# Two experts found by a sort of the eight logits and a search for their places, and the lists of turns written anew

## The chip, the cores and the metric

One core of one Trainium2 chip runs the whole program. The metric is the device time of one execution in microseconds (us). A core has five engines that run side by side, each with its own instruction queue: TensorE (PE, matrix products and transposes into PSUM), VectorE (DVE), ScalarE (ACT, exp, gelu, copies with a scale), GpSimd (POOL) and SyncE (SP, which issues the DMAs). They wait for each other by semaphores only.

## The reference, cut to what matters

Four layers stand one behind the other, each with a cross attention (16 heads, a context of 154 tokens) and a feed-forward part; the residual stream `x` is 4 batches x 1024 rows x 256. The feed-forward parts of layers 1 and 3 are mixtures of eight small experts, of which each row uses two:

```python
# layer 1
logits = x @ gate_w.T                       # [rows, 8]
scores = softmax(logits)
weights, idx = top_k(scores, 2)             # the scores themselves are the weights
base = x @ W_lin.T + b_lin
t = einsum('nd,nkdr->nkr', x, left[idx])    # rank 4 for each expert
out = base + sum_k weights[k] * (t[k] @ right[idx[k]])

# layer 3
probs = softmax(t @ gate_w.T)               # [rows, 8]
topw, topi = top_k(probs, 2)
topw = topw / sum(topw)
weights = sum(one_hot(topi, 8) * topw)      # each row's weight for each expert
out = einsum('te,etd->td', weights, out_e)  # out_e: a gated unit with a rank-16 part for each expert
```

A tie goes to the expert with the lower number.

## The kernel before, in words

The 4096 rows are cut into 16 pieces of 256. Four streams `S[0]` to `S[3]` each own one piece of a batch at a time and carry it through all four layers; then they store it and load the piece of the next batch. A stream's data stay in SBUF, 128 partitions x 2 rows. PSUM has eight banks: four form the `quad`, in which attention scores are made for one stream at a time, the others are handed out bank by bank.

The work of a stream is cut into some 30 kinds of stages (`norm`, `turn`, `qp`, `sc`, `mx`, `s2`, `ex`, `pv`, `out`, `gate1`, `top1`, `tl`, `lin`, ...). A stage has a part on each engine that it needs. Within an engine the instructions run strictly in the order in which they were written, so the order of the stage parts of the four streams is what can be chosen. That order is fixed at build time by two things:

- `TURN` holds one string of digits for each engine: the k-th digit says from which stream the k-th stage part of this engine comes (1688 digits for PE, 1190 for ACT, 1206 for DVE, 592 for POOL, 34 for SP).
- `parts` holds a planned duration of every stage on every engine (`pe`, `dve`, `act`, `pool`, in ns). `orders()` walks the strings with these durations. Because the strings give the streams, the durations decide nothing of the order within an engine: they decide which bank a stage gets, and how many `fill` matmuls go into the PE queue. Where the plan sees PE wait for more than 450 ns, it puts a `fill` there: matmuls of an identity (L992) whose result nobody reads, sized to three quarters of the planned wait.

The stages that the change touches are these.

Layer 1. `gate1` on PE (L1370) makes base, the eight logits and the rank-4 products in one go, 296 columns for each of the two row groups, in two banks. `gate1` on DVE takes the largest logit of each group (L1968, `tensor_reduce` from PSUM) and subtracts it (L1971); that lets ACT take the exp of the eight (L1659). `top1` on DVE then finds the two experts, as a one-hot over eight for each: `first` (L1950 to L1953) marks the places with the value 0, multiplies them by the row 8, 7, ..., 1 (`rev`, a slice of the tile `w_first`), takes the largest and compares it with `rev` to get the first expert alone, and then puts that place far below the rest; L1981 takes the largest of what is left; `second` (L1959 to L1962) does the same marking for it. Each of these operations waits for the one before it by the semaphore `d_own` (the helper `own`). The rest of `top1` (L1983 to L1991) adds the two one-hots, weighs the exps, divides by their sum and multiplies the rank-4 products, into the tile `tl`. `tl` on PE (L1378) transposes that, ACT copies it (L1669), `lin` on PE (L1386) multiplies it by `right` into the two banks of base, and `lin` on DVE (L2001) adds all of it to `x`.

Layer 3. `gate3` on PE (L1442) makes only the logits, 16 columns in one bank. `gate3` on DVE takes the largest (L2065), subtracts it (L2066), runs `first` and takes the second largest (L2068), which lets ACT take one exp (L1664). `top3` on DVE runs `second` and then four operations that make the two weights (L2077 to L2080). `mw` on POOL (L948, L950) spreads one-hots and weights over 128 columns, PE transposes them (L1453) and ACT copies them to SBUF (L1705); then come `exa`, eight rounds `h1`, `h2`, `hw`, `back` on all engines, `e3` (L2118, L2121) and `f3` (L1508).

Each of the four stages runs 16 times: four streams, four batches.

Of the kernel before, what the change touches and what calls it, by code (L numbers as in the profile page):

```python
# [29 lines left out]
def build(nc, d, out):  # L30
# [5 lines left out]
    with ctx:  # L36
# [20 lines left out]
        def res(name, shape, dt=f32):  # L57
# [5 lines left out]
        FMQ, GATES, FMQB, SGN, FMV, FMVB, NEGC, SELC, TM, BD2, REV, BQ, BK, NW, UPB, G3 = (  # L63
# [3 lines left out]
        gates, fmqb, sgn, fmv, fmvb, negc, selc, tm, bd2, rev, nw, upb = (  # L67
            GATES, FMQB, SGN, FMV, FMVB, NEGC, SELC, TM, BD2, REV, NW, UPB)
# [105 lines left out]
        for i in range(NS):  # L174
# [64 lines left out]
            s.gs = [s.g8[:, k, :, :] for k in range(6)]  # L239
            s.tops = [s.sm[:, 8 + k, 0:2] for k in range(6)]  # L240
# [16 lines left out]
        def parts(name, of):  # L257
# [12 lines left out]
                   "down": 700, "gate1": 620, "top1": 2800, "lin": 800, "q1": 2390, "w1": 660, "am": 2170, "fin": 830,  # L270
                   "q2": 1420, "w2": 400, "gate3": 1440, "top3": 1515, "exa": 1600, "h1": 885, "h2": 800, "e3": 1120,
# [106 lines left out]
        def turns(s):  # L378
# [35 lines left out]
            for b in range(4):  # L414
# [161 lines left out]
                "0323023032323232002020221221202201003303100331331302121212012121032021202302322013221321303213300323"  # L576
                "1301202030201203123121301310012002011321013210203231300232202201321300103133233030122013122010010230"
                "2102113102311212330202020301322131210301301300233033203020232102101013001010031303313212102121100211"
                "2021302303230000032313003000000000000032001312230032210131211112111111111111111212101331103021202302"
                "0201221022223022312222212210200222210102211032313012323333233323333333233333233130302322122302013032"  # L580
                "3032003213213301203131030210103123013100230021021312310113102032312300220220321310302301331032310320"
                "1012210031020210233211103321102010222030221323101301131003003323303020232102101201300101003331301231"
                "2101211210103123203203021030302000000030002000100300032013200202132321010301112111111111111111111133"
                "2113021203202022012210222212223231222122102002122202012103231303212333233323332333230333333332022331"
                "3221230323031031230313102301303201020310120312313010203002102321311311021230031302022022032131030230"
                "3313310320201121020031020210132312110323110201022203022132310301301130120303323023203201210101031000"
                "1303033130121120121121012021302302301300200203003003030103100300000002022300322101213011112111111111"
                "1111112111020131312320202030212210232021232122012002222222222100122123031303133232133333333333323323"
                "3323133023202212323032013032032123010213030210331032101031023130120200310231211301131020323123002202"
                "2103231030203331331203020112102003102021013231211021112330202020301322131213031012300303032223030230"  # L590
                "1201010130010103033130312112012112101202120323020310000300020303000030003003020130022100322321013121"
                "1121121111111111111111133113212232222222222222222222232232232333333333333333333333333333",
            "ACT":
                "0001030032122312020023003233011123211200310031202212201213133033010322021213213233032001202101310031"
                "3030222102102100133331212321200022021031133011302232303012100020113032300230111312201010130320223210"
                "1021023120330331000303300000000000120121323211211111111111131212102130020320021212212323222222200302"
                "2201010313122323313333333303333310202232210230310220213012303101332113213302300203210311301013303202"
                "2102120010313321231321020022032301311301032122300213010002103133020302113112010103213022203312110301"
                "2032302130303010300000000001002021213231002101111111130111121113203220232122121222232222200302212001"
                "3103123223313333330303333332201222323103012013211033200321302113123302300202330131113030103022210210"  # L600
                "2010333132231211200022023301311301032212300213010020130233021030111312110300321023023212110202103230"
                "1303000030303010011000000202323211211101131121111111121020032203012212321232222002202222231001330132"
                "1332323133333333333001202233223012002121201230103031332112310332302020331011310013303202201210201033"
                "3123213211200022032301131101302322303121002001013203230030113112010130231023022312110022102303103000"
                "300303003000010200102231231211211211211111111311133222222222223222222323333333333333333333",
            "DVE":
                "3233203213023230232020232020313231023103120202223200111122121233223223220023023321130303001212110020"
                "0332121020303110032131201122030320213122313130200023302123301000110103112310312032200212102230210301"
                "1332323130310132100322003212301303200021300300000010003031100121211122111111111112121030312130232200"
                "2220232212212212212003200212130333032333332333323323113331122223322030303310103300331221110202003312"  # L610
                "0120131030023213120211003202131221331020233003203200100111001313101213032002211202230210320112333332"
                "1313010120032320013123302101000002000302000300303101012021011221111111111111132321302301220220221222"
                "1322122132220020021132003332332333232333333331132321122322333000331010330013322111202033002121001301"
                "0032323120121103020231221331102023300230320010011100132301312101322002121223021030110333233231310101"
                "2300223001231203130020100200330031003100000001221111212111111111112210013231033222002202121322122222"
                "2120230200303201133333333332332332331123321213223223030003110333001332211120200033120120131000323231"
                "2012101032023122133110202302030123301000110113021321013232012002122030210301133233321331010120022330"
                "0212130100021033000020300303000301012210221111121111211111111331233222222222222222233232333333333333"
                "333333",
            "POOL":  # L620
                "0100100102301132012123200203133102210302313201100322012302113020323101301232002013011332010200303201"
                "2300001000311121111211112200231213022220221233030233331032333213123022300103132013210203301211030230"
                "2120323121300032310113200210301332210103020013321100002000031120110121011112232312221232012223300210"
                "2333323333132123023102003131032321030032110023212101032313000232130112320010321032130103200021301300"
                "1200300011211212111110202301132320222221230302033333231332132312102230010330322110303120103012320121"
                "03231302002313101232201003013132010232000103000301200031112211111211123222232222233333333333",
            "SP": "0300030102300000123000010230001023",
# [1105 lines left out]
        def dve_program(e):  # L1733
# [551 lines left out]
```

## Time and profile before

| | us |
|---|---|
| median of 3 runs | 2492.91 (2492.24 to 2493.57) |
| the profiled execution's own time | 2491.67 |
| its span, first to last instruction | 2489.6 |
| PE busy | 2375.2 |
| DVE busy | 1325.7 |
| ACT busy | 1144.9 |
| POOL busy | 854.1 |

The span is some 2 us shorter than the execution's own time. Busy times are unions of the instructions of one engine; each engine also waits, and only waits of the engine that bounds a stretch cost time. The program falls into four batches, each of which passes layers 0 to 3 with the four streams a little apart; so every view that goes over the whole span mixes stretches with different limits.

### The profile page before, as it was taken

What the parts mean: (1) busy time and instruction counts of PE and PEld (TensorE: products, weight loads), DVE (VectorE), ACT (ScalarE), POOL (GpSimd) and SP (SyncE); (2) the same over time, 40 slices, a digit from 0 to 9 for tenths busy, and PEclk for the clock granted to TensorE, in tenths of its full rate; (3) what the DMA queues carried; (4) which work ended last, traced back from release to release, by engine and by line L of the source; (5) the groups of instructions that cost most, each with busy time, mean ns of one, the idle gap of its engine ahead of it and who ended that gap; (6) DMA issues with size and microseconds to landing.
All of it is one profiled execution on the core that took longest, in us unless ns stands there. A gap on an engine that the chain in (4) does not pass through costs nothing.

```text
span 2489.6 us, 51976 instructions
## 1 busy us (share of the span) xinstructions
PE 2375.2 (95%) x21666; PEld 1601.6 (64%) x21666; DVE 1325.7 (53%) x2974; ACT 1144.9 (46%) x1756; POOL 854.1 (34%) x1546
## 2 busy tenths in 40 slices
PE   8999989999999988999999998899999999899999
PEld 4676544777777644567777754467777765447777
DVE  6544776545433577644543367764544346865442
ACT  5534567323344548723325445762323545683211
POOL 1332332434332332334432233333433223334342
PEclk9999999999999999999999999999999999999999
DMA  3200002000000000000000000000000000000000
GB/s 137 89 12 1 13 19 84 1 9 10 10 10 13 13 2 15 2 9 8 3 9 21 1 13 1 13 1 10 9 10 10 13 2 13 1 2 1 1 9 9
DMA packets 16614, 37.86 MB, mean 15 GB/s; under 512 B 1472, under 2 KB 11520, under 8 KB 15360
## 3 DMA queue, kind: packets, MB, share of 16 engines
q1 hardware_dynamic: 16384, 34.55, 4.0%
q8 instruction: 174, 2.85, 0.5%
q14 instruction: 56, 0.46, 0.1%
HBM read 29.78 MB, written 4.19 MB: 14 GB/s over the span
## 4 chain that ended last, share of the span: by engine, by line
PE 74%; DVE 9%; ACT 9%; issue 5%; POOL 2%; DMA 0%; DVEq 0%; ACTq 0%; POOLq 0%
PE P L1475 9%; PE P L1262 5%; PE P L1508 5%; PE P L1359 5%; PE P L1484 4%; PE P L1476 4%; PE P L1493 4%; PE P L1334 4%; PE P L1240 4%; PE P L1153 4%; PE P L1346 4%; ACT ET L1633 3%; DVE mx L1882 3%; PE P L1269 3%; PE P L1149 2%
## 5 line engine op out<-in xcount | busy, mean ns | idle before, releaser
L1882 DVE TENSOR_REDUCE mx<-P 128x8 f32<-128x1232 f32 x256 | 367.2, 1434 | 210.8 <-PE P L1158 86.1
L1475 PE MATMUL P<-Et,w 128*128 128x256 f32 x1024 | 265.7, 382 | 0.1
L1475 PEld LDWEIGHTS P<-Et,w 128*128 128x128 f32 x1024 | 192.1, 190 | 60.2 <-issue 33.4
L1926 DVE SCALAR_TENSOR_TENSOR x<-P,w_first,x 128x512 f32<-128x512 f32 x96 | 71.8, 748 | 273.9 <-PE P L1359 98.9
L1587 ACT ACTIVATE Et<-x,sm 128x256 f32<-128x256 f32 x256 | 139.2, 594 | 156.4 <-POOL sm L885 155.7
L1633 ACT ACTIVATE ET<-P 128x2048 f32<-128x2048 f32 x96 | 180.2, 1877 | 40.7 <-PE P L1252 20.4
L1711 ACT ACTIVATE gu<-P 128x256 f32<-128x256 f32 x128 | 49.0, 383 | 299.7 <-PE P L1476 280.0
L1153 PE MATMUL P<-KB,R 32*128 32x308 f32 x1536 | 155.7, 474 | 20.6 <-DVE mx L1882 10.6
L932 POOL TENSOR_TENSOR R<-R 128x512 f32<-128x512 f32 x48 | 60.8, 1268 | 319.9 <-DVE R L1918 319.9
L2098 DVE SCALAR_TENSOR_TENSOR gu<-gu,P 128x256 f32<-128x256 f32 x128 | 53.8, 420 | 215.8 <-ACT gu L1711 215.6
L1240 PE MATMUL P<-R,KB 32*128 32x256 f32 x2048 | 162.8, 405 | 3.6 <-DVE mx L1882 3.6
L1262 PE MATMUL P<-ET,VB 128*32 128x256 f32 x2048 | 146.1, 392 | 13.9 <-ACT ET L1633 5.9
L879 POOL TENSOR_SCALAR sm<-mv 128x2 f32<-128x2 f32 x96 | 18.4, 192 | 395.9 <-DVE mv L1877 394.1
L1476 PE MATMUL P<-gu,b 128*128 128x256 f32 x512 | 152.4, 380 | 0.0
L903 POOL TENSOR_TENSOR x<-x,w_bias 128x512 f32<-128x512 f32 x112 | 141.8, 1268 | 28.7 <-ACT Et L1587 28.6
L992 PE MATMUL P<-identb 128*128 128x512 bf16 x486 | 134.8, 389 | 6.6 <-POOL mg L852 4.6
L1484 PE MATMUL P<-gu,b 128*128 128x256 f32 x512 | 134.4, 385 | 0.0
L1346 PE MATMUL P<-Et,wup 128*128 128x256 f32 x512 | 124.1, 388 | 0.1
L956 POOL TENSOR_TENSOR Et<-Et,gu 128x512 f32<-128x512 f32 x48 | 60.9, 1268 | 173.8 <-DVE Et L2105 173.8
L1240 PEld LDWEIGHTS P<-R,KB 32*128 32x128 f32 x2048 | 81.6, 187 | 59.0 <-issue 33.7
L1508 PE MATMUL P<-w_w,R 128*128 128x256 f32 x512 | 118.3, 385 | 0.8 <-DVE R L2121 0.4
L1359 PE MATMUL P<-wdn,R 128*128 128x256 f32 x512 | 114.6, 382 | 1.8 <-ACT R L1653 1.8
(290 smaller groups left out, 4968.2 us busy)
## 6 DMA issues: line engine op xcount, KB each, us to landing
kvw<-in_wkv SPq DMA_DIRECT2D x12, 672.0 KB, 4.0
x<-in_x SPq DMA_DIRECT2D x16, 256.0 KB, 2.8
out<-x SPq DMA_DIRECT2D x16, 256.0 KB, 2.1
w<-in_w SPq DMA_DIRECT2D x2, 1024.0 KB, 8.6
w<-in_wexp SPq DMA_DIRECT2D x1, 1028.0 KB, 8.8
w_w<-in_wcon SPq DMA_DIRECT2D x1, 1024.0 KB, 11.0
w_w<-in_m3t SPq DMA_DIRECT2D x1, 1024.0 KB, 6.7
w<-in_w1q SPq DMA_DIRECT2D x1, 1024.0 KB, 10.0
```

The lines of the kernel that those rows point to most:

```text
L903: e.tensor_tensor(s.x[:], s.x[:], gb[:, k:k + 1, :].broadcast_to([128, 2, 256]), ALU.add).then_inc(s.g_x, 1)
L1153: t = e.matmul(quad[:, g, 0:2 * NK], s.QT[G4[g], u, rows], K[G4[g], 2 * u:2 * u + 2, :], start=True, stop=l >= 2)
L1240: e.matmul(quad[:, g, cols], K[G4[g], j, 0:128], s.QT[G4[g], j if l == 0 else u, :], start=a == 0, stop=False, skip_group_check=True)
L1262: t = e.matmul(o[G4[q], :], of(q), ET[:, g, 256 * a:256 * a + 256], start=start, stop=False, skip_group_check=True)
L1346: t = e.matmul(o[:, 256 * (j % 2):256 * (j % 2) + 256], wup[:, c, 128 * j:128 * j + 128], s.xT[:, c, :], start=c == 0, stop=c == 1)
L1359: t = e.matmul(o[:, 256 * i:256 * i + 256], s.hT[:, j, 128 * i:128 * i + 128], wdn[:, j, :], start=j == 0, stop=j == 7)
L1475: e.matmul(o, wm[:, c, js], s.xT[:, c, :], start=n == c == 0, stop=False, skip_group_check=True)
L1476: t = e.matmul(o, bm[:, js], U[:, 2 * n, :], start=False, stop=False, skip_group_check=True)
L1484: t = e.matmul(P[:, k, 256 * n:256 * n + 256], bm[:, js], U[:, 2 * n + 1, :], start=False, stop=n == 1, skip_group_check=True)
L1508: e.matmul(o, s.G[:, j, rows], w2[:, j, :], start=j == 0, stop=False)
L1633: e.activation(ET[:].rearrange("p g c -> p (g c)"), quad.rearrange("p g c -> p (g c)"), ACT.Exp, bias=mb1[:, b:b + 1] if l == 1 else 0.0). ...
L1882: e.tensor_reduce(s.mx[:, i, :, 2 * u:2 * u + 2], quad[:, :, 0:2 * NK].rearrange("p g (a k) -> p g a k", a=2), AX.X, ALU.max).then_inc(q_d, 1)
```

## The change

The chain of comparisons goes. In its place stand two instructions of VectorE for each row group: `max` writes the eight values of a row in falling order, and `max_index` writes the places at which given values stand. One comparison of the places with the row 0, 1, ..., 7 (`kth`, in the place of `rev`) then makes both one-hots of both groups at once. The places are written into the slot 3 of the tile `g8`, read as unsigned integers (`s.at`).

```diff
-            def first(s):
-                g, m, sh = s.gs, s.tops, [128, 2, 8]
-                rv = rev[:].unsqueeze(1).broadcast_to(sh)
-                own(e.scalar_tensor_tensor(out=g[3], in0=g[0], scalar=0.0, in1=rv, op0=ALU.is_equal, op1=ALU.mult))
-                own(e.tensor_reduce(m[3], g[3], AX.X, ALU.max))
-                own(e.tensor_tensor(g[1], rv, m[3].unsqueeze(2).broadcast_to(sh), ALU.is_equal))
-                own(e.scalar_tensor_tensor(out=g[5], in0=g[1], scalar=-1e38, in1=g[0], op0=ALU.mult, op1=ALU.add))
-            def second(s):
-                g, m, sh = s.gs, s.tops, [128, 2, 8]
-                rv = rev[:].unsqueeze(1).broadcast_to(sh)
-                own(e.tensor_tensor(g[3], g[5], m[2].unsqueeze(2).broadcast_to(sh), ALU.is_equal))
-                own(e.tensor_tensor(g[3], g[3], rv, ALU.mult))
-                own(e.tensor_reduce(m[3], g[3], AX.X, ALU.max))
-                own(e.tensor_tensor(g[2], rv, m[3].unsqueeze(2).broadcast_to(sh), ALU.is_equal))
+            def ranked(s, of):
+                for i in range(2):
+                    e.max(s.gs[5][:, i, :], of[i]).then_inc(d_own, 1)
+                e.wait_ge(d_own, C.up(d_own, 2))
+            def found(s, of):
+                for i in range(2):
+                    e.max_index(s.at[:, i, :], s.gs[5][:, i, :], of[i]).then_inc(d_own, 1)
+                C.up(d_own, 2)
+            def chosen(s):
+                e.wait_ge(d_own, C.at(d_own))
+                sh = [128, 2, 2, 8]
+                own(e.tensor_tensor(s.g8[:, 1:3, :, :], kth[:].unsqueeze(1).unsqueeze(1).broadcast_to(sh),
+                                    s.at[:, :, 0:2].rearrange("p i k -> p k i").unsqueeze(3).broadcast_to(sh), ALU.is_equal))
             def gate1(s, k0, k1):
-                g, m = s.gs[0], s.tops[0]
+                g = s.gs
+                logits = [P[:, k, 256:264] for k in sorted((k0, k1))]
                 e.wait_ge(s.p_d, C.up(s.p_d))
-                for i, k in enumerate(sorted((k0, k1))):
-                    e.tensor_reduce(m[:, i:i + 1], P[:, k, 256:264], AX.X, ALU.max).then_inc(d_own, 1)
-                e.wait_ge(d_own, C.up(d_own, 2))
-                for i, k in enumerate(sorted((k0, k1))):
-                    t = e.tensor_scalar(g[:, i, :], P[:, k, 256:264], m[:, i:i + 1], None, ALU.subtract)
+                ranked(s, logits)
+                for i in range(2):
+                    t = e.tensor_scalar(g[0][:, i, :], logits[i], g[5][:, i, 0:1], None, ALU.subtract)
                 t.then_inc(s.d_a, 1)
                 C.up(s.d_a)
+                found(s, logits)
             def top1(s, k0, k1):
                 lo = [P[:, k, 264:296] for k in sorted((k0, k1))]
                 g, m = s.gs, s.tops
-                e.wait_ge(s.d_a, C.at(s.d_a))
-                first(s)
-                own(e.tensor_reduce(m[2], g[5], AX.X, ALU.max))
-                second(s)
+                chosen(s)
                 own(e.tensor_tensor(g[5], g[1], g[2], ALU.add))
                 e.wait_ge(s.a_d, C.up(s.a_d))
...
             def gate3(s, k):
                 g, m = s.gs, s.tops
-                logits = P[:, k, 0:16].rearrange("p (i n) -> p i n", i=2)
+                logits = [P[:, k, 8 * i:8 * i + 8] for i in range(2)]
                 e.wait_ge(s.p_d, C.up(s.p_d))
-                own(e.tensor_reduce(m[0], logits, AX.X, ALU.max))
-                own(e.tensor_tensor(g[0], logits, m[0].unsqueeze(2).broadcast_to([128, 2, 8]), ALU.subtract))
-                first(s)
-                e.tensor_reduce(m[2], g[5], AX.X, ALU.max).then_inc(s.d_a, 1)
+                ranked(s, logits)
+                found(s, logits)
+                e.tensor_tensor(m[2], g[5][:, :, 1], g[5][:, :, 0], ALU.subtract).then_inc(s.d_a, 1)
                 C.up(s.d_a)
             def top3(s):
                 m = s.tops
-                e.wait_ge(s.d_a, C.at(s.d_a))
-                second(s)
+                chosen(s)
                 e.wait_ge(s.a_d, C.up(s.a_d))
```

The planned durations of the four stages on DVE change with it, and all five strings of `TURN`:

```diff
-                   "down": 700, "gate1": 620, "top1": 2800, "lin": 800, "q1": 2390, "w1": 660, "am": 2170, "fin": 830,
-                   "q2": 1420, "w2": 400, "gate3": 1440, "top3": 1515, "exa": 1600, "h1": 885, "h2": 800, "e3": 1120,
+                   "down": 700, "gate1": 900, "top1": 1700, "lin": 800, "q1": 2390, "w1": 660, "am": 2170, "fin": 830,
+                   "q2": 1420, "w2": 400, "gate3": 800, "top3": 950, "exa": 1600, "h1": 885, "h2": 800, "e3": 1120,
...
-            "SP": "0300030102300000123000010230001023",
+            "SP": "0300030012300000123000001230002013",
```

The order of the stages of one stream on one engine stays as it was; what changes is how the streams are laid between each other. Counted from the strings, with each stage followed by its stream and its number in it, these stage parts stand at another place than before: 924 of 1688 on PE, 612 of 1190 on ACT, 617 of 1206 on DVE, 382 of 592 on POOL and 6 of 34 on SP, spread over all four batches. Nine in ten of these are moved by one to five places, a few by up to 30. Between `gate1` and `tl` of the same stream PE had 84 stages of other streams in all 16 cases together, and has 78 after.

## Rows read from the trace of the kernel before

**Rows 1.** The page: busy time by engine, and PE in 40 slices.
```profile
PE 2375.2 (95%) x21666; PEld 1601.6 (64%) x21666; DVE 1325.7 (53%) x2974; ACT 1144.9 (46%) x1756; POOL 854.1 (34%) x1546
...
PE   8999989999999988999999998899999999899999
```

**Rows 2.** Windows of 100 us: us, busy (and count) by engine, granted PE clock, DMA.
```profile
500.00:600.00 100.00, 98.87 (x696) 73.65 (x689) 45.85 (x111) 31.35 (x57) 39.27 (x61) 1.00 0.04 12
...
800.00:900.00 100.00, 94.31 (x987) 59.13 (x985) 56.19 (x139) 52.01 (x75) 27.97 (x62) 1.00 0.03 8
900.00:1000.00 100.00, 88.72 (x985) 49.70 (x985) 75.06 (x161) 68.85 (x83) 33.73 (x73) 1.00 0.03 10
```

**Rows 3.** The same windows for the fill matmuls, line 992 alone: the sum.
```profile
sum 2500.00, PE 134.83 PEld 44.67; mean PE 5.39 PEld 1.79
```

**Rows 4.** The page: the chain that ended last, by engine.
```profile
PE 74%; DVE 9%; ACT 9%; issue 5%; POOL 2%; DMA 0%; DVEq 0%; ACTq 0%; POOLq 0%
```

**Rows 5.** Timeline of DVE in one `top1` of batch 2: start, us, instruction.
```profile
1451.48 0.17 DVE L1951 TENSOR_REDUCE sm<-g 128x2 f32<-128x16 f32 x1
...
1453.14 0.17 DVE L1983 TENSOR_TENSOR g<-g 128x16 f32<-128x16 f32 x1
```

**Rows 6.** Groups of DVE by line and shape: busy, mean ns of one | idle before.
```profile
L1950 DVE SCALAR_TENSOR_TENSOR g<-g,w_first 128x16 f32<-128x16 f32 x32 | 10.8, 339 | 0.7
L1960 DVE TENSOR_TENSOR g<-g,w_first 128x16 f32<-128x16 f32 x32 | 9.3, 291 | 1.1
L1962 DVE TENSOR_TENSOR g<-w_first,sm 128x16 f32<-128x16 f32 x32 | 8.3, 260 | 1.1
L1952 DVE TENSOR_TENSOR g<-w_first,sm 128x16 f32<-128x16 f32 x32 | 7.6, 237 | 1.1
L1991 DVE SCALAR_TENSOR_TENSOR R<-P,sm,g 128x32 f32<-128x32 f32 x32 | 6.6, 247 | 0.6
L1953 DVE SCALAR_TENSOR_TENSOR g<-g 128x16 f32<-128x16 f32 x32 | 5.6, 175 | 1.1
L1968 DVE TENSOR_REDUCE sm<-P 128x1 f32<-128x8 f32 x32 | 3.7, 157 | 5.1 <-PE P L1370 5.1
```

**Rows 7.** Timeline of DVE: `gate1` of stream 0 in batches 1 to 3, counted from 0.
```profile
844.59 0.24 DVE L1968 TENSOR_REDUCE sm<-P 128x1 f32<-128x8 f32 x2 [0.74 <-PE P L1370]
...
1449.91 0.24 DVE L1968 TENSOR_REDUCE sm<-P 128x1 f32<-128x8 f32 x2 [0.71 <-PE P L1370]
...
2048.95 0.24 DVE L1968 TENSOR_REDUCE sm<-P 128x1 f32<-128x8 f32 x2 [0.74 <-PE P L1370]
```

**Rows 8.** Waits of all engines: who <- whom, us in total, times, longest.
```profile
ACT g L1659 <- DVE g L1971: 22.8, 13, 3.9
```

**Rows 9.** The chain in order of time, at two `top1`: start, us, what.
```profile
236.08 0.98 DVE g L1950
...
2097.03 0.09 DVE g L1950
```

**Rows 10.** Groups of PE by line: the transpose behind `top1`.
```profile
L1378 PE MATMUL P<-ident,R 128*64 128x128 f32 x16 | 4.5, 284 | 7.0 <-DVE R L1991 5.4 <-ACT R L1647 1.4
```

**Rows 11.** Waits of PE alone, columns as in rows 8.
```profile
PE P L1153 <- ACT ET L1633: 7.9, 18, 2.1
```

**Rows 12.** Timeline of all engines at the last `gate3` and `top3`.
```profile
2417.57 0.17 DVE L2065 TENSOR_REDUCE sm<-P 128x2 f32<-128x16 f32 x1
...
2419.05 1.13 PE L1493 MATMUL P<-gu,w_a 128*128 128x512 f32 x2
...
2420.01 2.32 PE L992 MATMUL P<-identb 128*128 128x512 bf16 x10
...
2421.12 0.17 DVE L2077 TENSOR_SCALAR sm<-sm 128x2 f32<-128x2 f32 x1
...
2421.80 0.42 DVE L2118 SCALAR_TENSOR_TENSOR R<-P,gu 128x256 f32<-128x256 f32 x1
```

**Rows 13.** A window of 10 us in batch 3, columns as in rows 2.
```profile
2130.00:2140.00 10.00, 6.38 (x76) 2.40 (x69) 8.53 (x28) 4.41 (x6) 3.59 (x9) 0.83 0.00 0
```

More of the change, by code:

```diff
@@ L581, in build @@
[L581 to L585, printed above, removed]
@@ new lines, in build @@
+                "0232303230323232202002220120222101000331003331013313112212120122302120232032122013220132302313300323"
+                "1310320210230201021321301310021002011321013210203231300232202210231030103133233032021013122010010230"
+                "2101211301213212330202020301322131213010130030230333030202321012021013000110303310321231212011121010"
+                "2103230230320000303210003000300300020030100022103032210121311121111121121111111111113310130021020203"
+                "2221021202212222321223022021200222210210211032313102323233323333323333333332033313023220322123032301"
@@ new lines, in build @@
+                "3032032031332130101321030210103120313100230021023211231011310032313020220220132303010230331331203102"
+                "1122100031020210312321103231120102202030221323101301110303003323303020232102102101300011030331301231"
+                "1201211201103213023020210302003200303000000130000000002321300230122132130111211111111111112111121133"
+                "1103021202030201222102220221212221232322012002222010212103230313323123323333233333230333233323221330"
+                "3022123032303103103120313321320301030210102132031310203002310231211311021320302310022022032131030230"
@@ new lines, in build @@
+                "3313312030201101221003102021031212310323112010230022021232310130101310320330320323023201012011031000"
+                "1303033130121120121121012021203203203130030003200030023000000300010030201320322101213011211101111111"
+                "1111121111133211301020320203221202102221223122102002222222221202201230113012312333323323333233333333"
+                "2333310330232212230210310312303213002312331303020310102031210301312012003032113011321020323130202202"
+                "2103231030230331132320301011220100310202102113231021112330202020301322131210303101203003323223030230"
@@ new lines, in build @@
+                "1201101030100130303313011212012112110202103230230230203003103003000230000000100030022301022321013121"
+                "1111211211111111111111133113212232222222222222222222222332232333333333333333333333333333",
+            "ACT":
+                "0000300212321213020023003203131111232012300312012210220213133033130021202132321233023002102101310031"
+                "3300222102102010133332123112200022021013130131302232303012100020113033020302113112010310231022202331"
+                "2110201032033031000303030000001200010022313211211112111231121111111300320002021221212232232222200302"
+                "2201013013212123333333333333033031202202232330102210231332013011032112313302300203231011310031303022"
+                "2012001203133123121321200022023130131301021232300213010002103133020302113112010130231022203312101032"
+                "1032301203000330030100010000000223211123211011111121112111131230203020011222212222322232200022231001"
+                "1303312332123333333033033323210202232303101210132133201302031123123303200230233101113030130202202110"
+                "2003133123213211200022032130131301032312200213010200130323020130111312101300321023202312110202102303"
+                "1033030030030001200000001021323211230111110111121111211130230020233211222122222002222032221003031122"
+                "1233313333033333333301022232210321031102120321023303301213123032302010323011310031303022201210201033"
+                "1322313121200022023101331101302232303012100200112303230030111312101300312023023212110202103203303013"
+                "030300002000011000002321231211112121111131112111132322222232222222222233333333333333333333",
@@ new lines, in build @@
+            "DVE":
+                "2332313023203232023202020302132310032130120322121223001121212233223223202203302323113300001122110020"
+                "0332121020313100023131201212030320212123313130200020323123301000110103112130132031202021022301203201"
+                "1333233213012310122003300123201033020002100310300300030001011202111221111121111121111033012130220222"
+                "3012221222302212212302000212303303233233333332333321131323112222332033003110330300133221112020200331"
+                "1020130100332321020121103022131221331020233002303201000111001313101213032010222102230120320113332332"
+                "1310310123003220031120121330020002030000030000033011012211122111111111111212103031210202322320022121"
+                "2221322122230200023210331303323333233233233331312321221323203300311030303013322111202033002121001310"
+                "0032323120121100320321122313102023300230320101001100132131021310322002121220301302110332333321310101"
+                "2030223002121320331010000203003000030003011001221211112111111111111200323133021202202202123122122222"
+                "2213020200201033332332313333323333321133311222232230330013130303003132121102000332121020131000323213"
+                "1202110230302112231310202330200123301000110103112320113220302021122030130121033233332131010120022330"
+                "0232032310120001130030003000000301102201221111121111111111211331232223222222222222233223333333333333"
@@ new lines, in build @@
+                "0210132321300320310132010210301232101330022001301030001020031121121111112202301120232220231223300233"
+                "2303332331123203121030103330232112030210310023211002312310320321301021320010310321201302032001330120"
+                "0001003011211211111120023231220022212322133002203333333312131202312230031030312103020313210012321230"
+                "02311032023130102230101203103321013022000310320100000301112211111111223223232222223333333333",
+            "SP": "0300030012300000123000001230002013",
@@ L2260 @@
         fm2, rows(np.concatenate([v["g_xattn"], v["g_ffn"]])), np.tile(v["L0_xattn_fm_b"], 8), sgn, spread(fmT, 8),
-        rows(v["L0_xattn_fm_b"]), negc, selc, tm, bd2, rows((8.0 - np.arange(8)).astype(np.float32)), bq, bk,
+        rows(v["L0_xattn_fm_b"]), negc, selc, tm, bd2, rows(np.arange(8).astype(np.float32)), bq, bk,
         v["L3_ffn_norm_w"].reshape(2, 128).T, v["L0_ffn_up_bias"].reshape(8, 128).T, kt(v["L3_ffn_gate_w"].T))], 1)
```

51 lines of the change are left out of this document (6 added, 45 removed).

## The prediction

> **What bounds the kernel now.** I read the page first, then windows of 100 us, then the chain, and last the single groups and timelines. PE is busy 95% of the span, DVE 53% [rows 1]. But PE's share is an average over unlike stretches: in layers 3 and 0 of a batch PE is full (98.87 of 100 us), in layers 1 and 2 it is busy 94.31 and 88.72 us while DVE rises to 56.19 and 75.06 [rows 2]. And part of PE's busy time is no work: the fill matmuls take 134.83 us over the whole program [rows 3], so that with the 114 us of idleness (2489.6 less 2375.2) some 249 us of PE's queue are not work. In layers 1 and 2 the end is therefore set by chains that run over DVE, ACT and PE in turn; DVE holds 9% of the chain that ended last [rows 4]. The change shortens DVE's part in layer 1, where that counts, and in layer 3, where PE is full and it mostly does not.
>
> **Layer 1, `top1`.** Nine instructions go: L1950 to L1953, L1981, L1959 to L1962. Each waits for the one before. From the start of L1951 to that of L1983 are eight such steps in 1.66 us [rows 5], 0.2075 us each, nine are 1.87 us. That is the quiet case. The four that read the tile `w_first` have means of 339, 291, 260 and 237 ns, against 175 for L1953, their like without it [rows 6]: they are held up now and then, by 107 ns in the mean. Four of them in a stage add 0.43 us. Removed: 2.30 us.
>
> Added, in `top1`: one comparison of 32 elements that reads `w_first` too. Its nearest rows are L1962 (260, with the hold-ups in it) and L1991 (247, 32 elements) [rows 6]; with the step's gap of some 35 ns I take 0.30 us, and for the doubled size and the hold-ups 0.10 more: 0.40 us. Ends: 0.21 (the quiet step) and 0.56, twice L1991 with its gap twice.
>
> Added, in `gate1`: the two `max` stand where the two reductions stood (L1968, 157 ns each from PSUM [rows 6]) and write eight values in place of one; I give the pair 0.05 us more. The two `max_index` are new work behind the subtraction. The trace of before has no such instruction. From below they are two small PSUM reads that don't wait for each other: not under zero, since they occupy the queue, and the pair L1968 takes 0.24 us together [rows 7], so 0.12 each. From above I allow four times the dearest mean of a small operation here, L1968's 157 ns: 0.63 each. I take 0.20 each, next to the lower end, because the nearest row (eight values from PSUM) is the lower one: 0.40 us. What is queued behind them on DVE is a `mx` of another stream in most cases, and PE's next scores wait for the quad which that frees.
>
> One wait comes nearer: `top1` needs ACT's exp. Before, 2.30 us of searching lay between; now 0.40 of `max_index` and 0.40 of comparison do. In 13 of 16 cases ACT already sat idle for the subtraction [rows 8], takes the exp at once and is done in 0.2 us; in the other three it may still be in other work, and DVE, with all that stands behind `top1`, would wait up to 1 us. I count this as nothing, and it widens the range by 3 us.
>
> So a layer 1 stage costs DVE 2.30 - 0.40 - 0.05 - 0.40 = 1.45 us less, between 0.4 (the new prices at their upper ends) and 1.85. It is even only when a `max_index` costs 0.92 us.
>
> How much of it shows? The chain runs through the removed instructions in 9 of the 16 `top1` stages, the first at 236.08, the last at 2097.03 [rows 9]. All of the saving in all nine, with nothing else late in its place, would be 9 x 1.45 = 13.0 us. From the other side: PE itself stands idle before the transpose behind `top1` for 7.0 us in all, 5.4 of them for L1991 [rows 10]; if the stage only ended earlier and helped nobody but its own transpose, 5.4 us would go. Between 5.4 and 13.0 I take 8.5, somewhat below the middle: of the DVE time that frees, a part is also given to the `mx` of other streams (75.06 of 100 us busy in the next window), but where one wait on the quad ends earlier, PE's wait for ACT's exp of the quad stands behind it (18 times, 7.9 us before one line of the scores alone [rows 11]).
>
> **A rule on the price.** `max_index` writes its places with an instruction that the trace of before does not show, and the rows give only its neighbours. The Trainium skill (VectorE: DVE Perf Modes, section Two Vector instructions with no wait between them) says that the search for places is two instructions, one that loads the values sought and one that finds them. No run here shows it yet. By that rule 64 searches would be 128 instructions; at the 157 ns of the reduction [rows 6] and end to end a search would be 0.31 us in place of 0.20, the layer 1 stage would save 1.23 instead of 1.45 us, and the sum would be smaller by about 1.3 us. That is the rule that speaks against the change: in layer 1 it puts 5 instructions in for the 9, where the lines of the program show 3.
>
> **Layer 3.** `gate3` had seven steps of 0.2075 (1.45 us) and has two `max` (0.29 with the wait), two searches (0.40) and a subtraction (0.20): 0.56 less. `top3` loses four steps (0.83) and gains the comparison (0.40): 0.43 less. With two of the hold-ups of 0.107 us gone from each, that is 1.4 us less on DVE in each of 16 places. Fifteen I cost at nothing: PE is full there (98.87 us) [rows 2] with the work of the other streams, and a shorter DVE part only waits longer for its turn. If that cover were gone, it would be up to 1.4 us a place. The sixteenth is the last `gate3`, at 2417.57. There PE has little left: it burns fills of 2.32 us (from 2420.01) while DVE goes through the search, and L1950 and L1952 are held up, so that 3.55 us pass from L2065 to L2077 [rows 12]. After the change this is some 1.3 us. But `e3` of the stream before (L2118) stands behind it and starts at 2421.80; it needs the last `back`, the matmul L1493 at 2419.05 that takes 1.13 us. So L2118 can start no sooner than about 2420.3: 1.5 us earlier. I count 1.5 us.
>
> **The lists.** 2541 stage parts on the five engines stand elsewhere, most by one or two places. On POOL and SP nothing is added or removed, only reordered. What a list is worth can be read from the batches of before, which do the same work in other orders: `gate1` of stream 0 starts at 844.59, 1449.91 and 2048.95 [rows 7], two batches of 605.3 and 599.0 us. Two orders of the same work thus lie 6 us apart in a batch. Over four batches a new list may bring or take some 8 us, part of it through the clock: where PE stood idle in the fourth batch, its granted clock was 0.83 over 10 us, a third of which at 1.2 in place of 2.4 GHz [rows 13], which costs 1.7 us each time. I see no reason for a sign and take 0. The fills go with the planned waits; since the planned `top1` falls from 2800 to 1700, there will be somewhat fewer of them, and that is in the 8.5.
>
> **Sum.** 8.5 + 1.5 + 0 = 10.0 us. The profiled execution of before took 2491.67 us (span 2489.6); it becomes 2481.7. The median shown, 2492.91, lies 1.24 above the profiled execution, so I forecast 2482.9 for the median, say 2483. Its own range: 2474 to 2488.
>
> **Rivals.** *The gain is absorbed.* The saving in `top1` meets the next wait, on ACT's exp of the quad or on the `mx` queue; or the banks come free earlier only to wait. For it: nobody but PE counts, and PE waits directly for `top1` for only 5.4 us [rows 10]. Against it: nine `top1` on the chain. With 2 us of the 13.0 left and 1 us from the tail, less a list that loses 1: 2491. Chance 0.17.
>
> *The lists gain as well.* The new lists use the freed DVE time in layers 1 and 2 to bring matmuls nearer: then the full 13.0, the tail, 0.5 in layer 3 and some 5 to 8 of the list term: 2492.9 - 21 = 2472. For it: 249 us of PE's queue are idle or filled, and PE has six stages fewer between `gate1` and `tl`. Against it: a stage put earlier waits in the queue if DVE is not done. Chance 0.18.
>
> *The plan is wrong, and the kernel slower.* The strings were written for planned durations, 900 and 1700 ns for layer 1. Where the real ones are longer, PE's strict queue stands before a `tl` or `sc` that the plan holds ready. The price: 16 layer 1 places and 16 of layer 2 with 0.6 us more of PE waiting each (the idle before L1378 is 0.44 a place now [rows 10]) are 19 us, less the 10 gained: 2502. It decides from the point at which the new order loses 10 us more than the old, or at which a `max_index` costs over 0.92 us. For it: so many places moved, and 924 on PE. Against: nine in ten moves are of few places, and both `gate1` and `top1` together are planned 820 ns shorter while I work out 1450, so the plan errs on the safe side. Chance 0.15.
>
> The forecast itself has 0.50. Faster by over 0.2% (5 us, about what a measurement of this kernel can tell from no change) means under 2487.9: nearly all of the forecast's 0.50, less 0.03 at its upper edge, and the 0.18: 0.65. Within 0.2%: 0.17, 0.03 and a little of the last: 0.21. Slower: 0.14. The range holds the second rival and the upper end of the first, and stops short of the slow one: 2468 to 2497.
>
> **What would show it.** In the changed profile: `max` near 160 ns and `max_index` at 0.12 to 0.31 us a search; DVE's busy sum down by some 40 us (16 x 1.45 and 16 x 1.4 less the gaps between instructions); the chain with less than half of its former time in the lines of the search; idleness before the `tl` transpose under 4 us in all; PE full as before in layer 3; at the last `gate3` 1.5 us less until `e3`. Fills fewer than 134.8 us. It would be wrong if a search cost 0.5 us or more, if PE's waits for `mx` and for ACT's exp grew by what those for L1991 fell, or if the batches drew apart from 599 to 605 us without any reason in these lines, for then the lists decide and not the search.

## The result, and the profile after

| | us |
|---|---|
| median before, same chip | 2493.22 |
| median after, 4 runs | 2465.13 (2465.08 to 2465.3) |
| ratio | 0.9889 (0.9877 to 0.9902) |
| span of the profiled execution | 2463.5 (before 2489.6) |

28.1 us less; 10 were forecast, and the time lies under the range of 2468 to 2497. The page of the changed kernel, where the lines are one or two numbers higher:

```profile
PE 2361.8 (96%) x21643; PEld 1592.1 (65%) x21643; DVE 1289.6 (52%) x2855; ACT 1149.6 (47%) x1761; POOL 850.9 (35%) x1546
...
PE   8999989999999989999999999999999999899999
...
PE 78%; ACT 8%; DVE 8%; issue 3%; POOL 2%; DMA 0%; DVEq 0%; POOLq 0%; ACTq 0%
...
L993 PE MATMUL P<-identb 128*128 128x512 bf16 x463 | 126.0, 388 | 6.3 <-POOL mg L853 4.8
```

The reader is to hold it against [rows 1, 3, 4]. PE's busy time fell by 13.4 us, though its work is the same, and its idleness by 12.7 (2463.5 - 2361.8 = 101.7 against 114.4). Of the 13.4, 8.8 are fills (134.8 to 126.0); the other 4.6 I put down to the clock: the granted clock has a mean of 0.996 after and 0.992 before. DVE's busy time fell by 36 us. So three things are less: waiting, fills, and time at the low clock.

The new instructions, in the groups of DVE by line and shape (busy, mean ns | idle before), to be held against [rows 6]:

```profile
L1963 DVE TENSOR_TENSOR g<-w_first,g 128x32 f32<-128x32 f32 x32 | 10.7, 336 | 0.2
L1956 DVE FIND_INDEX8 g<-g,P 128x8 uint32<-128x8 f32 x64 | 9.8, 164 | 0.0
L1950 DVE MAX8 g<-P 128x8 f32<-128x8 f32 x64 | 7.7, 161 | 29.7 <-PE P L1443 24.6 <-PE P L1371 5.0
...
L1956 DVE MATCH_VALUE_LOAD g<-g,P 128x8 f32 x64 | 5.0, 79 | 0.6
```

`max` takes 161 ns. The search is two instructions, 79 and 164 ns, and they overlap, as the timeline of the last `gate3` shows (the one of [rows 12]):

```profile
2395.26 0.25 DVE L1950 MAX8 g<-P 128x8 f32<-128x8 f32 x2 [1.13 <-PE P L1443]
2395.55 0.09 DVE L1956 MATCH_VALUE_LOAD g<-g,P 128x8 f32 x1
2395.62 0.17 DVE L1956 FIND_INDEX8 g<-g,P 128x8 uint32<-128x8 f32 x1
2395.71 0.07 DVE L1956 MATCH_VALUE_LOAD g<-g,P 128x8 f32 x1
2395.76 0.17 DVE L1956 FIND_INDEX8 g<-g,P 128x8 uint32<-128x8 f32 x1
2395.85 0.14 DVE L2066 TENSOR_TENSOR sm<-g 128x2 f32<-128x2 f32 x1
2395.96 0.68 DVE L1963 TENSOR_TENSOR g<-w_first,g 128x32 f32<-128x32 f32 x1
2396.68 0.17 DVE L2074 TENSOR_SCALAR sm<-sm 128x2 f32<-128x2 f32 x1
...
2397.51 0.42 DVE L2115 SCALAR_TENSOR_TENSOR R<-P,gu 128x256 f32<-128x256 f32 x1
```

Both searches occupy the queue for 0.30 us, from 2395.55 to 2395.85; I had 0.40. From the first `max` to L2074 it is 1.42 us, where it was 3.55.

Where along the execution was the time won? The start of `gate1` of stream 0 in the four batches, to be held against [rows 7]; the first of them was at 234.11 before:

```profile
228.41 0.23 DVE L1950 MAX8 g<-P 128x8 f32<-128x8 f32 x2
...
829.25 0.24 DVE L1950 MAX8 g<-P 128x8 f32<-128x8 f32 x2
...
1429.43 0.25 DVE L1950 MAX8 g<-P 128x8 f32<-128x8 f32 x2 [1.46 <-PE P L1371]
...
2025.36 0.23 DVE L1950 MAX8 g<-P 128x8 f32<-128x8 f32 x2
```

5.7 us are won before the first search is run at all, 15.3 by batch 1, 20.5 by batch 2, 23.6 by batch 3, 26.1 at the end. The first number cannot be the search. It is the lists, which I had put at 0. These are single executions, and those of the kernel before lay up to 6.5 us apart on one chip (2489.45 to 2495.91); so a us or two between two traces says little, and the experiments go by medians.

### The profile page after: what moved, and what is told of

It reads as the page before. It is cut to its first block, busy times and chain, and to the rows that moved or that the text cites. A ratio compares the mean times of both kernels' runs of the same rounds, so it can differ in the third digit from the quotient of the medians.

```text
span 2463.5 us, 51816 instructions
## 1 busy us (share of the span) xinstructions
PE 2361.8 (96%) x21643; PEld 1592.1 (65%) x21643; DVE 1289.6 (52%) x2855; ACT 1149.6 (47%) x1761; POOL 850.9 (35%) x1546
## 4 chain that ended last, share of the span: by engine, by line
PE 78%; ACT 8%; DVE 8%; issue 3%; POOL 2%; DMA 0%; DVEq 0%; POOLq 0%; ACTq 0%
PE P L1476 9%; PE P L1263 5%; PE P L1335 5%; PE P L1360 5%; PE P L1241 5%; PE P L1509 5%; PE P L1485 4%; PE P L1477 4%; PE P L1154 4%; PE P L1494 4%; PE P L1347 4%; ACT ET L1634 3%; DVE mx L1883 3%; PE P L1270 3%; PE P L1122 3%
## 5 line engine op out<-in xcount | busy, mean ns | idle before, releaser
L993 PE MATMUL P<-identb 128*128 128x512 bf16 x463 | 126.0, 388 | 6.3 <-POOL mg L853 4.8
```

## The experiments

Times are medians of 4 to 11 executions. Differences in the table, and where runs on unlike chips are compared, are against the kernel before on the same chip (2492.82, 2493.27 and 2492.24 us for e1 to e4, e5 to e8 and e9 to e12). "Old" and "new lists" are the strings of `TURN`, "durations" the planned ones, which set fills and banks.

| run | lists | durations | search L1 | search L3 | median | difference |
|---|---|---|---|---|---|---|
| e1_search_only | old | old | new | new | 2482.28 | -10.5 |
| e9_oldlists_l1 | old | old | new | old | 2484.13 | -8.1 |
| e2_lists_only | new | new | old | old | 2495.07 | +2.3 |
| e5_new_l1 | new | new | new | old | 2475.53 | -17.7 |
| e6_new_l3 | new | new | old | new | 2488.48 | -4.8 |
| the change | new | new | new | new | 2465.13 | -28.1 |

**One part alone.** e1 is the changed kernel with the strings and durations of before, e2 the kernel before with those of the change:

```diff
 e1 (on the changed kernel)
-                   ... "gate1": 900, "top1": 1700, ... "gate3": 800, "top3": 950, ...
+                   ... "gate1": 620, "top1": 2800, ... "gate3": 1440, "top3": 1515, ...
...
+        TURN = { ... the five strings of before ... }
 e2 (on the kernel before): the same two edits the other way round
```

> The new search (max, max_index, one comparison) with the strings of TURN and the planned durations of before. The measured change is -28 us. Theory A (the order of the streams gives most of it): the search alone gives the 10 us that were forecast for it, about 2483. Theory B (the search gives most of it, since the quad and the banks come free earlier everywhere): 2470 or less. Theory C (each needs the other): 2488 to 2493.

2482.28 us, ratio 0.9958 (0.9945 to 0.9971). Theory A's number, and that of the prediction without its list term.

> The old search with the new strings and the new planned durations. Theory A: about 2475, some 18 us less than before, since the gain of the lists does not hang on the search. Theory B: 2488 to 2495. Theory C: 2490 or above, since the new strings put tl and sc of other streams where only the shorter search lets them run; then the two single gains sum to far less than 28.

2495.07 us, ratio 1.0012 (1.0003 to 1.002): the lists alone make the kernel slower, by little. Theory A falls in this half: the new lists are worth -17.6 us on top of the new search (-28.1 against -10.5) and +2.3 on top of the old one. Theory C had the sign here and not in e1. The search pays by itself; the lists pay only with it.

Why, PE's idle time before the `tl` transpose says; line numbers differ, the shape is the one of [rows 10]. e1, e2 and the changed kernel in turn:

```profile
L1379 PE MATMUL P<-ident,R 128*64 128x128 f32 x16 | 4.7, 291 | 2.5 <-ACT R L1648 2.1 <-ACT R L1609 0.3
```

```profile
L1378 PE MATMUL P<-ident,R 128*64 128x128 f32 x16 | 4.6, 287 | 21.1 <-DVE R L1991 15.8 <-ACT R L1647 5.1
```

```profile
L1379 PE MATMUL P<-ident,R 128*64 128x128 f32 x16 | 4.7, 294 | 6.0 <-ACT R L1648 3.7 <-DVE R L1990 2.1
```

Under the old order PE idled 7.0 us there [rows 10]; the short search takes that to 2.5, none of it for the last DVE instruction of `top1`, so at this place a still shorter one has little to win. The new order puts `tl` nearer behind `gate1`, by 6 stages in 84. With the old search PE stands there for 21.1 us, with the new one for 6.0: 15 of the 25.4 us by which PE idles longer in e2 than in the changed kernel (127.1 against 101.7). The clock falls with the waiting: in the 100 us from 1447 the lists alone were granted 0.93, the changed kernel 0.98 (columns as in [rows 2]):

```profile
1447.00:1547.00 100.00, 87.55 (x941) 50.01 (x940) 64.72 (x157) 47.38 (x67) 32.17 (x70) 0.93 0.03 8
```

```profile
1447.00:1547.00 100.00, 90.36 (x936) 50.98 (x929) 72.79 (x165) 57.60 (x78) 33.05 (x66) 0.98 0.01 2
```

Over the whole program this second price is small here: without the fills PE is busy for 2238.2 us in e2 and for 2235.8 after the change.

**The fills.** e3 is e1 with the new durations.

> The new search with the old strings, but the new planned durations, so that only the sizes of the fills and some banks differ from the kernel with the search alone. If fills of too great a size held PE up: 2 to 4 us less than the search alone. If they cost nothing and only hold the clock up: within 1 us of it.

2480.39 us, 1.9 less than e1. The two intervals (0.9953, 0.994 to 0.9966; e1's above) overlap, so a gain is not shown.

**Only the start from the new lists.** e4 has the new search and durations and takes the new strings only up to the first `gate1`; e7 does the same to the kernel before, and e8 goes on with the new strings until `gate1` of batch 1. In short (the kernels have the strings written out):

```diff
+ cut = {"PE": 147, "ACT": 101, "DVE": 107, "POOL": 38, "SP": 0}      # e4, e7
+ cut = {"PE": 561, "ACT": 395, "DVE": 400, "POOL": 188, "SP": 7}     # e8
+ TURN = {e: new[e][:cut[e]] + old[e][cut[e]:] for e in new}
```

> The new search and the new durations; the new strings up to the first gate1 (some 230 us, where no search runs at all), the old ones from there on. In the two traces that point lies at 231.0 and 225.3 us. If what is won before it is kept to the end: 5 to 6 us less than with the old strings throughout. If it is given back in the waits of the first layers 1 and 2: less than 2 us.

2472.3 us, 8.1 less than e3, ratio 0.9924 (0.9912 to 0.9937). The start's 5.7 us are kept; that they grow to 8 is not shown by these two medians, whose executions lie 7 and 5 us apart.

> The kernel before, with only the strings up to the first gate1 (147, 101, 107, 38 and 0 stage parts on PE, ACT, DVE, POOL and SP) taken from the new lists; the old search, the old durations. If the gain of the start (8 us with the new search) has nothing to do with the search, as no search runs in that stretch: 2485 to 2487. If it needs the short search behind it: 2490 or more.

2484.86 us, -8.4, ratio 0.9963 (0.9949 to 0.9976). The strings of the start are worth 8 us with either search: 147 of 1688 stage parts of PE bring half of what the lists bring. In the trace of e7 `gate1` of stream 0 starts at 229.66, 837.49, 1442.68 and 2041.83: 4.5 us earlier than before in batch 0, and 7.1 to 7.2 in batches 1 to 3, so the gain is kept to the end, and some 2.6 of it come between the first `gate1` and batch 1.

This also says where the old search spoils the lists. Behind the start they cost 10.7 us with it (+2.3 in e2 against -8.4 in e7) and bring 7.6 with the new one (-28.1 against -20.5 in e4). e7 has the old durations and e2 the new ones; e3 puts those at no more than some 2 us.

The start is the stretch in which the weights of the butterfly are folded (`grow`, `near`, `wide`). The window from 25 to 50 us, first before, then e7:

```profile
25.00:50.00 25.00, 18.56 (x175) 11.22 (x174) 21.41 (x37) 15.94 (x39) 4.41 (x8) 0.88 0.01 3
```

```profile
25.00:50.00 25.00, 21.91 (x229) 11.84 (x227) 23.13 (x45) 19.42 (x42) 2.47 (x6) 1.00 0.03 10
```

PE is busy 3.4 us more of the 25, DVE and ACT are busier by 1.7 and 3.5, and the clock stays up.

> The new search and durations; the new strings until gate1 of stream 0 in batch 1, the old ones from there on. With only the start it was 2472.3, with all new strings 2465.1. In the traces the new strings win 2 us more up to that point and lose 2 behind it in batch 2. If the rest of the gain is made in batch 0: 2467 to 2470. If it is made in batches 1 to 3: 2472.

2471.27 us, ratio 0.9908 (0.9893 to 0.9922): 22.0 below before where e4 was 20.5, so 1.5 less, within what can be told. The remaining 6.1 us to the change are made in batches 1 to 3; at which places, these runs don't tell.

**Which layer's search.** e5 and e6 put the old functions back for one layer (with `rev` made from `kth` once at the start), under the new lists; e9 does the same as e5 under the old ones.

```diff
 e5, e9: gate3 and top3 as before;   e6: gate1 and top1 as before
+            e.tensor_scalar(rev[:], kth[:], -1.0, 8.0, ALU.mult, ALU.add).then_inc(d_own, 1)
```

> The changed kernel with the new search in layer 1 (gate1, top1) and the old one in layer 3 (gate3, top3). It lies between the changed kernel (2465) and the new lists with the old search in both layers (2495). Theory A (the new lists were drawn for the short search of layer 1, where PE waits): 2468 to 2472, since layer 3 gives only its tail of 1.5 to 3 us. Theory B (the order of layer 3 hangs on it as much): 2477 or more.

2475.53 us, ratio 0.9926 (0.9913 to 0.9939).

> The changed kernel with the new search in layer 3 and the old one in layer 1. Theory A: 2488 to 2493, nearly all of the 30 us lost. Theory B: 2483 or less.

2488.48 us, ratio 0.9977 (0.9967 to 0.9986). Layer 1's search is worth 20.0 us (e5 against e2) or 23.3 (the change against e6) under the new lists. But layer 3's is worth 7.1 (e6 against e2) or 10.4 (the change against e5), not 1.5; theory A's range for e5 is missed by 3.5 us, and each theory fails somewhere. PE's waits for the spread weights of layer 3 show 3.4 us of it (e5, then the change):

```profile
PE P L1455 <- POOL Et L952: 4.8, 5, 2.0
```

```profile
PE P L1454 <- POOL Et L951: 1.4, 2, 1.0
```

PE idles 9.1 us longer in e5 altogether (110.8 against 101.7), and no other wait differs by over 1.4 us, so the rest is spread thin and its cause stays open.

> The strings and planned durations of before, the new search in layer 1 alone, the old one in layer 3. With both layers it was 2482.3, 10.5 us below before. Theory A (the two terms of the prediction, 8.5 for layer 1 and 1.5 for layer 3, were right under the old strings): 2484 to 2486. Theory B (layer 3 gives 6 us or more under any strings, as it did under the new ones): 2487 to 2490.

2484.13 us, ratio 0.9968 (0.9955 to 0.998). Under the old lists layer 1 gives 8.1 and layer 3 the other 2.4, beside terms of 8.5 and 1.5. The intervals of e9 and e1 overlap, so the 2.4 can't be told from nothing; the 7.1 and 10.4 can. The same instructions in layer 3 are worth little or 7 to 10 us, by the order of the streams around them.

**Small moves inside the stages.** e10 moves the searches of layer 1 from the end of `gate1` to the start of `top1`; e11 puts the subtraction of `gate3` ahead of its searches, with one semaphore more for the bank.

```diff
 e10
-                found(s, logits)           # end of gate1
+                found(s, [P[:, k, 256:264] for k in sorted((k0, k1))])   # start of top1
 e11, gate3
-                found(s, logits)                 # moved behind the subtraction
                 e.tensor_tensor(m[2], g[5][:, :, 1], g[5][:, :, 0], ALU.subtract).then_inc(s.d_a, 1)
                 C.up(s.d_a)
+                e.max_index(s.at[:, 0, :], s.gs[5][:, 0, :], logits[0]).then_inc(d_own, 1)
+                e.max_index(s.at[:, 1, :], s.gs[5][:, 1, :], logits[1]).then_inc(d_f, 1)
...
 e11, top3
+                e.wait_ge(d_f, s.f)
                 chosen(s)
```

> The changed kernel, but the two max_index of layer 1 stand at the beginning of top1 and not at the end of gate1. In 9 of 16 places DVE does other stages, mostly mx, between the two; these now come some 0.4 us earlier and the places 0.4 us later. If PE waits for mx more than for tl: 1 to 3 us less. If for tl (6.0 us of idleness before it): 1 to 3 us more. If neither: within 1 us of 2465.

2464.75 us, ratio 0.9886 (0.9871 to 0.9901).

> The changed kernel with the subtraction in gate3 ahead of the two max_index, so that ACT starts its exp some 0.5 us sooner; the bank is given back after the second max_index by a semaphore of its own. If the chain max, max_index, subtraction, exp, scaling is what PE's waits in layer 3 hang on: 1 to 4 us less than 2465. If the exp is hidden by the comparison on DVE: within 1 us.

2464.83 us, ratio 0.9892 (0.9877 to 0.9907). Both are the changed kernel's time. In e11 the exp is hidden, as the second half of its expectation says; in e10 neither wait bounds, or what `mx` wins `tl` loses, which this run doesn't tell apart.

**No fills.** e12 is the changed kernel with the line in `orders` left out that adds fills.

```diff
-                        lists["PE"].append(("fill", k, int(0.75 * (at - begun - 100.0) / 215.0)))
+                        pass
```

> The changed kernel without any fill matmuls (107 us of PE's queue that no work fills). If the fills only stand where PE waits in any case and the clock does not need them: 2460 to 2466. If they hold the clock up: dips of the granted clock from 7 to 20 or more, each costing 1.7 us of matmul work, and 2475 or more.

2500.1 us, ratio 1.0031 (1.0021 to 1.0042), 36 us more than with them (+7.9 against -28.1). A line of its page, and two windows, in which the changed kernel was granted 0.97 and 1.00:

```profile
PE 2292.6 (92%) x21146; PEld 1572.3 (63%) x21180; DVE 1288.6 (52%) x2855; ACT 1151.0 (46%) x1761; POOL 850.9 (34%) x1546
```

```profile
300.00:400.00 100.00, 77.58 (x870) 44.17 (x873) 70.83 (x157) 68.03 (x85) 31.05 (x70) 0.91 0.18 64
...
1500.00:1600.00 100.00, 80.66 (x897) 46.10 (x899) 70.49 (x155) 67.74 (x83) 29.05 (x63) 0.93 0.03 8
```

The mean granted clock falls from 0.996 to 0.978. That is 0.018 x 2496.6 = 45 us of full speed that PE was not granted, a part of it while it idled. PE's busy time tells more: without the fills it is 2292.6 us here and 2235.8 in the changed kernel (2361.8 - 126.0), so the same matmuls took 57 us longer; 24 came back, since PE's idle time and fills together fell from 227.7 to 204.0. The difference, 33, is that of the two spans. So waiting in this kernel has a second price, and a list that waits less saves both.

## Why the prediction was wrong

**The search's terms were right, its instructions nearly so.** Sum 10.0, measured 10.5 (e1, 7.2 to 13.7 by its interval); layer 1 8.5 against 8.1 (e9), layer 3 1.5 against 2.4, each known to some 3 us at best. A search was put at 0.20 us and holds the queue for 0.15; the comparison at 0.40 and has a mean of 0.34 with 0.03 of gap; `max` "near 160" is 161; DVE busy was to fall by 40 us and fell by 38 in e1 (1325.7 to 1287.5).

**The rule on the price.** The Trainium skill (VectorE: DVE Perf Modes, Two Vector instructions with no wait between them) was right that the search is two instructions: 64 rows of each are there. The 0.31 us that I worked out from it were not: the load takes 79 ns and the next instruction begins before it is over.

**Where the 10 us came was not as told, so the good sum is in part luck.** I spread layer 1's saving over nine places of the chain in all batches. With the old lists `gate1` of stream 0 starts at 234.35, 836.85, 1442.81 and 2040.50 in e1:

```profile
836.85 0.25 DVE L1950 MAX8 g<-P 128x8 f32<-128x8 f32 x2 [0.75 <-PE P L1371]
...
1442.81 0.25 DVE L1950 MAX8 g<-P 128x8 f32<-128x8 f32 x2 [0.72 <-PE P L1371]
...
2040.50 0.25 DVE L1950 MAX8 g<-P 128x8 f32<-128x8 f32 x2 [0.74 <-PE P L1371]
```

7.7 us are won by batch 1 [rows 7], 7.1 by batch 2, 8.5 by batch 3, and over 3 more in the tail. The two full batches gave 0.7 us together, as far as one trace of each kernel tells. In batch 1 the wait before one `tl` (1.1 us) did go, and as much was given back soon after, where the clock fell in e1 and not before. The same stretch of work, from one `w1i` matmul to the next but one (L1412 before, L1413 in e1), took 2.98 us before and 4.14 in e1:

```profile
1011.52:1014.50 2.98, 2.81 (x24) 1.10 (x24) 1.97 (x7) 1.72 (x1) 0.00 (x0) 1.00 0.00 0
```

```profile
1002.98:1007.12 4.14, 4.14 (x23) 1.35 (x22) 2.19 (x8) 1.49 (x1) 0.00 (x0) 0.59 0.00 0
```

**The step that failed is "I see no reason for a sign and take 0", the list term.** It is -17.6 us with the new search. Two reasons could have been found before. First, the lists begin before any search: the strings of the first 231 us bring 8 us (e7, e4). Of that stretch I had read only windows of 100 us, in which the first has PE busy for 87.17 us at a clock of 0.97; in finer ones the clock stood at 0.88 and PE idled 6.4 of the 25 us from 25 on. Second, the term is not independent of the others: behind the start the same lists are worth +10.7 or -7.6 us, by the search. I added the search's gain, measured on the old order, and the lists' gain, as if each were fixed; e1, e2 and the change show -10.5, +2.3 and -28.1. Under the old order PE seldom waited for the long search (7.0 us [rows 10]), so a shorter one could win little until the order asked for it earlier. My rival "the lists gain as well" had this mechanism, with six stages fewer between `gate1` and `tl`, but capped the search's part at 13 us and got 2472. Of the prediction's own signs of being wrong one came, if weakly: the batches of `gate1` of stream 0, 605.3 and 599.0 us before, are 600.2 and 595.9 after. And the idleness before the `tl` transpose, to be under 4 us, is 6.0.

**Layer 3 at nothing.** Not refuted under the old order (2.4 us in 16 places with the tail, near the noise), wrong under the new one (10.4). That PE is at 99% in a stretch [rows 2] only says that the order of before kept it so; nothing says that the order of after could without the short stage.

**The slow rival** asked for lists that lose 10 us more than the old ones. With the old search they lose 10.7 behind the start, made up to 2.3 by the start's gain (e7, e2); with the new one it didn't happen.

**The wait for ACT's exp**, counted as nothing, is 1.4 us in all (L1985 in the groups of DVE), so it was nothing.

## What to carry to other kernels

Where an order written by hand or by a search fits the durations of its stages, shortening a stage shows only what PE waits for today; the larger part comes with the order that uses it, and the two must be tried together (here -10.5 and +2.3 alone, -28.1 together). When a change carries a new order, read every stretch that it touches for idle time and low clock, the start too, in windows fine enough to show a single wait, before giving it a term of 0. And price a wait of TensorE with the clock that it costs.

## What the runs showed of the hardware

A small DVE instruction that reads two SBUF tensors is held until a running `tensor_tensor` of GpSimd is over, and so is a `tensor_scalar` on two SBUF columns. In the kernel before:

```profile
873.10 1.26 POOL L903 TENSOR_TENSOR x<-x,w_bias 128x512 f32<-128x512 f32 x1
873.21 1.18 DVE L1962 TENSOR_TENSOR g<-w_first,sm 128x16 f32<-128x16 f32 x1
```

174 ns of work take 1.18 us and end at 874.39, 0.03 after POOL's. I had tied this to the tile `w_first`. That was wrong: after the change the same happens to L2074, which adds 1 to two columns of the tile `sm` (mean 464 ns). In the trace after the change 36 DVE instructions of at most 32 columns took over 330 ns, the longest 1254, and each ended 17 to 51 ns behind a POOL `tensor_tensor` that ran beside it. `max` and the search, which read the logits from PSUM, never took more than 176 and 168 ns in 64 cases, though 11 and 23 of them began while a POOL `tensor_tensor` of 512 columns ran; reductions and reciprocals of small SBUF tiles were not held either (171 and 255 ns at most). The Trainium skill (GPSIMD Engine Reference, section Specifications, "SBUF interfaces") tells of contention with DVE instructions that have two SBUF inputs or run in a two-port mode. The trace agrees for those with two inputs; in which mode the `tensor_scalar` runs, no run here shows. The delay is here the whole rest of the POOL instruction.
